# A state-space layer and a ternary feed-forward layer on eight cores: the state's mean, the weights' splits and the ternary weight passes put in another order

## The reference

```python
# first: a state-space layer with one averaged state kernel per state
xn = layernorm(layernorm(x)) * ln_g + ln_b        # the inner layer normalizes once more
x_proj, z = split(xn @ W_in.T + b_in);  z = silu(z)
B_proj = x_proj @ W_B.T * dt.mean()               # 16 states
A_mean = exp(t * log_A).mean(over channels)       # for every distance t
x_mean = causal_conv(B_proj, A_mean)              # over the whole sequence
y = (x_mean @ W_C.T + D_skip * x_proj) * z
y = y @ W_out.T + b_out + residual
# second: a feed-forward layer, 1024 -> 4096 -> 1024
h = silu(conv3(act_quant(x) @ weight_quant(w1).T))
h = act_quant(h) @ weight_quant(w2).T
```

## Time and profile before

| | |
|---|---|
| timed runs, slowest core | 1612.19 us median of 3 (1611.64 to 1612.52) |
| profiled execution | 1623.43 us, span of its slowest core (core 3) 1621.9 us |
| spans of the eight cores | 1594.0 to 1621.9 us |
| mean granted TensorE clock | 0.900 to 0.909 of full speed |
| TensorE matmuls busy | 1281.8 us (79%) |
| VectorE, ScalarE busy | 893.1 us (55%), 830.9 us (51%) |
| DMA | 206.30 MB, mean 127 GB/s |

### The profile page before, as it was taken

One profiled execution on the slowest core, in us unless ns is written; L12 is line 12 of the kernel. 1 busy time (PEld: TensorE's weight loads), 2 busy tenths in 40 slices (PEclk: granted clock), 3 DMA queues, 4 the chain that ended last, 5 costly groups with the idle time before them and its releaser, 6 DMA issues.

```text
span 1621.9 us, 23432 instructions; the slowest of 8 cores (1594.0 to 1621.9 us)
## 1 busy us (share of the span) xinstructions
PE 1281.8 (79%) x8148; PEld 790.3 (49%) x8148; DVE 893.1 (55%) x1461; ACT 830.9 (51%) x1118; POOL 83.4 (5%) x149
## 2 busy tenths in 40 slices
PE   2785799898983998887898745654698899889887
PEld 1262344565443755554566313443464566466433
DVE  1177412522036354545443424898898899789842
ACT  1334454678962234333334433886766667577531
POOL 0100000000000111111010000000000000000000
PEclk9768889898996999999999967997899999999999
DMA  9745668686245344654666582542001201010011
GB/s 272 203 146 130 192 187 255 191 271 186 96 136 153 118 143 140 177 148 148 143 167 131 162 226 98 169 156 91 1 1 53 79 1 50 30 53 27 26 66 65
DMA packets 86984, 206.30 MB, mean 127 GB/s; under 512 B 8495, under 2 KB 50783, under 8 KB 82692
## 3 DMA queue, kind: packets, MB, share of 16 engines
q1 hardware_dynamic: 62948, 99.41, 22.4%
q0 software_dynamic: 23920, 105.39, 20.6%
HBM read 170.99 MB, written 33.79 MB: 126 GB/s over the span
## 4 chain that ended last, share of the span: by engine, by line
PE 42%; DVE 16%; DMA 14%; ACT 11%; issue 11%; SPq 4%; POOL 1%; DVEq 0%; ACTq 0%; POOLq 0%
PE psum L893 10%; PE psum L857 10%; PE psum L734 7%; PE psum L694 6%; DMA b_wcb<-w_t 3%; PE psum L647 3%; DMA f_xr<-x_rev_t 2%; DMA f_wr<-w_in_t 2%; DMA f_lab<-s_logat 2%; DMA b_gz<-s_sz 2%; DVE b_h L1347 2%; PE psum L766 2%; DVE b_ev L1299 1%; DMA s_xq<-b_xqs 1%; DVE f_xt L1215 1%
## 5 line engine op out<-in xcount | busy, mean ns | idle before, releaser
L857 PE MATMUL psum<-b_xq,b_w1q 128*128 128x257 f16 x2048 | 261.8, 283 | 88.0 <-DVE b_ev L1299 79.4
L857 PEld LDWEIGHTS psum<-b_xq,b_w1q 128*128 128x128 fp8e4 x2048 | 203.5, 101 | 151.9 <-issue 108.1
L893 PE MATMUL psum<-b_w2q,b_hq 128*128 128x512 fp8e4 x1024 | 244.7, 389 | 8.1 <-DVE b_x2t L1384 8.1
L893 PEld LDWEIGHTS psum<-b_w2q,b_hq 128*128 128x128 f16 x1024 | 102.7, 100 | 116.9 <-issue 20.0
L1612 ACT ACTIVATE b_hs<-b_hs,c_cw 128x512 f32<-128x512 f32 x128 | 92.0, 719 | 56.6 <-DVE b_hs L1307 56.5
L1304 DVE SCALAR_TENSOR_TENSOR b_hs<-b_ev,c_cw,b_hs 128x512 f32<-128x512 f32 x128 | 95.1, 743 | 20.1 <-ACT b_hs L1608 20.0
L1307 DVE SCALAR_TENSOR_TENSOR b_hs<-b_ev,c_cw,b_hs 128x512 f32<-128x512 f32 x128 | 96.1, 751 | 13.3
L734 PE MATMUL psum<-f_xh,b_wxh 128*128 128x256 bf16 (+1 forms) x512 | 72.3, 287 | 35.0 <-DVE b_y L1261 28.2
L1608 ACT ACTIVATE b_hs<-b_ev,c_cw 128x512 f32<-128x512 f32 x128 | 90.3, 707 | 13.0 <-DVE b_ev L1299 13.0
L1299 DVE TENSOR_TENSOR b_ev<-psum,b_rbc 128x514 f32<-128x514 f32 x128 | 87.4, 685 | 1.1 <-PE psum L857 1.1
L1261 DVE SCALAR_TENSOR_TENSOR b_y<-psum,c_dsb,b_gz 128x256 f32<-128x256 f32 (+1 forms) x64 | 30.8, 482 | 98.5 <-PE psum L734 40.3
(11 more groups left out here) (223 smaller groups left out, 1968.2 us busy)
## 6 DMA issues: line engine op xcount, KB each, us to landing
f_xr<-x_rev_t POOLq DMA_DIRECT2D x15, 2048.0 KB, 12.5
f_pk<-w_t POOLq DMA_DIRECT2D x16, 1024.0 KB, 8.3
b_wca<-w_t POOLq DMA_DIRECT2D x32, 512.0 KB, 4.3
b_wcb<-w_t POOLq DMA_DIRECT2D x32, 512.0 KB, 5.1
b_wck<-w_t POOLq DMA_DIRECT2D x16, 1024.0 KB, 5.1
f_xt<-xo_t SPq DMA_DIRECT2D x5, 1640.0 KB, 11.4
s_sz<-f_o SPq DMA_DIRECT2D x40, 205.0 KB, 5.8
f_wr<-w_in_t SPq DMA_DIRECT2D x16, 512.0 KB, 6.2
```

What stands on the lines that cost most here:

```text
L857: e.matmul(psum[:, o:o + 257], sb_w1q.ap()[:, k * DH + mh * 128:k * DH + mh * 128 + 128], x[:, c:c + 257], start=k == 0, stop=k == KD - 1) ...
L893: e.matmul(ps[4 + (t % 2) * 2 + half], sb_hq[i].ap()[:, kh * 128:kh * 128 + 128], sb_w2q.ap()[:, kh * D + half * 512:kh * D + half * 512 + ...
```

## The change

Four things, in the order of the diff's effect on the program.

- *The state's mean.* At item 36 VectorE copies it out of PSUM ahead of the splits 16 and 17, with four copies of all 128 partitions instead of sixteen of 17 rows. SP's stores are issued at item 36, not 37: four for the body and two for the edge columns instead of twelve in all. `v_xmstack` at item 38 now stands ahead of that item's splits. The W_C stack's loads move from item 29 to 17 (waiting for `XN_V`, with another place in memory), its operations from item 31 to 21, and the load of the output bias from item 36 to 32.
- *Weights to split.* Portions 8 to 23 are loaded by GpSimd and not by SP, into three buffers and not two, so load j waits for split j - 3. GpSimd's ternary chunks start after split 22.
- *Ternary weight in portions.* The four chunks of a tile are no longer in a row at its end: on VectorE the passes 0 to 3 stand after the first gate, after the first low half, after the third low half and after `v_quant`; on ScalarE after `a_ln1`, after the second high half, after `a_xq` and after `a_quant`. The same holds for the sum of |w2|.
- *w1's loads.* The eight loads of the ternary w1 are issued three in tile 14, three in 15 and two in 16, each time after that tile's `s_xqst`.

```diff
-AT_WCT = 29
+AT_WCT = 17
...
             if i == AT_WCT:
-                e.wait_ge(*G_V.end())
+                e.wait_ge(*XN_V.end())
...
-            if i == 30:
-                for j in (8, 9):
-                    s_wr(e, j)
-            if i in SPLIT_AT:
-                for j in SPLIT_AT[i]:
-                    if j + 2 < 24:
-                        s_wr(e, j + 2)
+            if i == AT_WSUM:
+                e.wait_ge(*G_V.end())
+                e.dma_start(out=sb_bo.ap(), in_=d_bout).then_inc(*BOLD.dma())
             if i == AT_TOEP:
-                e.wait_ge(*Q_T.end())
-                e.dma_start(out=sb_bo.ap(), in_=d_bout).then_inc(*BOLD.dma())
-            if i == AT_TOEP + 1:
                 e.wait_ge(*XM_V.end())
                 for g in range(4):
...
-                    src = bass.AP(x.tensor, x.offset, [[4 * NQ, 1], [NQ, 4], [1, 1]])
-                    e.dma_start(out=capd(s_xm, g * TLOC, [[1, 1], [4 * TLOC, 4], [1, 1]]), in_=src,
-                                allow_slow_non_contiguous=True).then_inc(*XMST.dma())
-                    src = bass.AP(x.tensor, x.offset + 16 * 4 * NQ + 1, [[4 * NQ, 1], [NQ, 4], [1, 1]])
-                    e.dma_start(out=capd(s_xm, g * TLOC + TOWN + 1, [[1, 1], [4 * TLOC, 4], [1, 1]]), in_=src,
+                x = sb_xmt.ap()
+                for o, col in ((0, 0), (16 * 4 * NQ + 1, TOWN + 1)):
+                    src = bass.AP(x.tensor, x.offset + o, [[32 * 4 * NQ, 4], [NQ, 4], [1, 1]])
+                    e.dma_start(out=capd(s_xm, col, [[TLOC, 4], [4 * TLOC, 4], [1, 1]]), in_=src,
                                 allow_slow_non_contiguous=True).then_inc(*XMST.dma())
...
             if t == 14:
                 e.wait_ge(*GT_T.at("item", NIT - 1))
                 for k in range(2):
                     e.wait_ge(*WQST[k].end())
-                for j in range(8):
-                    e.dma_start(out=caps(sb_w1q, j * 512, ...), in_=capd(s_wq, j * 512, ...))
...
+            if 14 <= t <= 16:
+                for j in range((t - 14) * 3, min((t - 13) * 3, 8)):
+                    e.dma_start(out=caps(sb_w1q, j * 512, ...), in_=capd(s_wq, j * 512, ...))
...
+            if i == AT_TOEP:
+                e.wait_ge(*XM_T.end())
+                for q in range(4):
+                    e.tensor_copy(sb_xmt.ap()[:, q * NQ:q * NQ + NQ], qbank(q * 4)[:, 0:NQ]).then_inc(*XM_V.up())
+            if i == AT_TOEP + 2:
+                v_xmstack(e)
             if i in SPLIT_AT:
...
+            v_wtern(e, t, 0)
             if t:
                 v_ln1(e, t - 1)
             if items:
                 v_gate(e, items[1])
                 v_gatelo(e, items[0])
+            v_wtern(e, t, 1)
...
+    def v_wtern(e, t, j):
+        c = 4 * t + j
+        if c < NCC:
+            e.wait_ge(*WCKLD[c % 2].at("cast", c))
+            e.tensor_scalar(wcc_of(c), wcc_of(c), wscale(1), MAGIC, op0=ALU.mult, op1=ALU.add).then_inc(*QW_V.up("tern", c))
...
+    def a_wpass(e, t, j):
+        c = 4 * t + j
+        if c < NCC:
+            e.wait_ge(*QW_V.at("tern", c))
+            if c > 1:
+                e.wait_ge(*WQST[c % 2].at(c - 2))
+            e.activation(sb_wq8.ap()[:, (c % 2) * 1024:(c % 2) * 1024 + 1024], wcc_of(c), AF.Sign,
+                         bias=sb_cst.ap()[:, 0:1], saturate=False).then_inc(*QW_A.up("tern", c))
+        elif c < 2 * NCC:
+            c -= NCC
+            e.wait_ge(*WCKLD[c % 2].at("sum", c))
+            a_wabs(e, 2, c, wcc_of(c), 56 + c)
...
+        for j in range(8, 24):                      # GpSimd
+            if j < 10:
+                e.wait_ge(*WS_V.at(7))
+            elif j == 10:
+                e.wait_ge(*CO_V.end())
+            else:
+                e.wait_ge(*WS_V.at(j - 3))
+            e.dma_start(out=wr_of(j), in_=d_wout[:, (j - 8) * D:(j - 7) * D] if j < 16 else d_win[j - 16]
+                        ).then_inc(*WR2LD[wr_slot(j)].dma(j))
         for k in range(3):
             e.wait_ge(*XZ[k].end())
         e.wait_ge(*ST_V.at("xm"))
+        e.wait_ge(*WS_V.at(22))
```

More of the change, by code:

```diff
@@ L224, in write_program @@
     sb_xm32 = nc.alloc_sbuf_tensor_at("f_xm32", [80, TLOC], F32, offset=zone4)
-    sb_wc32 = nc.alloc_sbuf_tensor_at("f_wc32", [80, D], F32, offset=nc.lookup_mloc(sb_cf).addr)
-    sb_bo = nc.alloc_sbuf_tensor_at("f_bo", [33, D], F32, offset=nc.lookup_mloc(sb_q2).addr)
+    sb_wc32 = nc.alloc_sbuf_tensor_at("f_wc32", [80, D], F32, offset=nc.lookup_mloc(sb_q2).addr)
+    sb_bo = nc.alloc_sbuf_tensor_at("f_bo", [33, D], F32, offset=nc.lookup_mloc(sb_cf).addr)
+    sb_wr2 = nc.alloc_sbuf_tensor_at("f_wr2", [128, D], F32, offset=nc.lookup_mloc(sb_raw).addr)
     place[0] = base
@@ L349, in write_program @@
     WRLD, WS_V, WS_A = [sig("wraw_loaded0"), sig("wraw_loaded1")], sig("wsplit_vector"), sig("wsplit_scalar")
+    WR2LD = [sig(f"wraw2_loaded{k}") for k in range(3)]
     WM_V = sig("wscaled_vector")
@@ L530, in sync @@
                 s_xqst(e, (t - 3) // 2)
+            if 14 <= t <= 16:
+                for j in range((t - 14) * 3, min((t - 13) * 3, 8)):
+                    e.dma_start(out=caps(sb_w1q, j * 512, [[KD * DH, 128], [DH, KD], [1, 512]]),
+                                in_=capd(s_wq, j * 512, [[NCK * 2048, 128], [DH, KD], [1, 512]])).then_inc(*W1LD[j].dma())
         e.wait_ge(*XQST.end())
@@ L558, in s_xt, with wr_slot, wr_of, wr_loaded @@
                     in_=capd(d_xt, n * TC, [[KD * TLOC, 128], [TLOC, KD], [1, TC]])).then_inc(*XTLD[n % 2].dma(n))
+    def wr_slot(j):
+        return j % 2 if j < 8 else (j - 8) % 3
+    def wr_of(j):
+        return sb_wr2.ap() if wr_slot(j) == 2 else sb_wr.ap()[:, wr_slot(j) * D:wr_slot(j) * D + D]
+    def wr_loaded(j):
+        return (WRLD if j < 8 else WR2LD)[wr_slot(j)].at(j)
     def s_wr(e, j):
@@ L562, in s_wr @@
             e.wait_ge(*WS_V.at(j - 2))
-        src = d_win[8 + j] if j < 8 else d_wout[:, (j - 8) * D:(j - 7) * D] if j < 16 else d_win[j - 16]
-        e.dma_start(out=sb_wr.ap()[:, (j % 2) * D:(j % 2) * D + D], in_=src).then_inc(*WRLD[j % 2].dma(j))
+        e.dma_start(out=wr_of(j), in_=d_win[8 + j]).then_inc(*WRLD[j % 2].dma(j))
     def s_gz(e, q):
@@ L976, in vector @@
                 e.tensor_copy(sb_amt.ap(), ps[5][0:16, 0:128]).then_inc(*AM_V.up())
-            if i == AT_WCT + 2:
+            if i == AT_WCT + 4:
                 v_wcstack(e)
@@ L987, in vector @@
                     v_wlo(e, j)
[L988 to L995, removed]
         v_bout(e)
@@ L1011, in vector @@
                 v_gatelo(e, items[0])
+            v_wtern(e, t, 1)
+            if items:
                 v_gate(e, items[2])
@@ L1018, in vector @@
                 v_gatelo(e, items[2])
+            v_wtern(e, t, 2)
+            if items:
                 v_gatelo(e, items[3])
@@ L1021, in vector @@
                 v_quant(e, t - 1)
[L1022 to L1026, removed]
+            v_wtern(e, t, 3)
         v_wsum(e, 2)
@@ L1101, in v_wmul @@
     def v_wmul(e, j):
[L1103 to L1107, removed]
+        e.wait_ge(*wr_loaded(j))
+        w = wr_of(j).rearrange("p (k m) -> p k m", k=KD)
+        e.tensor_tensor(w, w, caps(sb_dbc, (j - 16) * 128, [[D, 128], [0, KD], [1, 128]]), op=ALU.mult
+                        ).then_inc(*WM_V.up(j))
     def v_wsum(e, wi):
@@ L1192, in v_wlo @@
     def v_wlo(e, j):
-        r = (j % 2) * D
         e.wait_ge(*WS_A.at(j))
-        e.tensor_tensor(split_of(j, 1), sb_wr.ap()[:, r:r + D], split_of(j, 0), op=ALU.subtract).then_inc(*WS_V.up(j))
+        e.tensor_tensor(split_of(j, 1), wr_of(j), split_of(j, 0), op=ALU.subtract).then_inc(*WS_V.up(j))
     def split_of(j, part):
@@ L1456, in scalar @@
                 a_ln1(e, t - 1)
-            for q in items[1:3]:
+            a_wpass(e, t, 0)
+            for q in items[1:2]:
+                a_gatehi(e, q)
+            a_wpass(e, t, 1)
+            for q in items[2:3]:
                 a_gatehi(e, q)
@@ L1464, in scalar @@
                 a_xq(e, t - 3)
+            a_wpass(e, t, 2)
             if t:
                 a_quant(e, t - 1)
[L1468 to L1478, removed]
+            a_wpass(e, t, 3)
         a_xq(e, 14)
@@ L1540, in a_whi @@
     def a_whi(e, j):
-        r = (j % 2) * D
-        e.wait_ge(*WRLD[j % 2].at(j))
+        e.wait_ge(*wr_loaded(j))
         if 2 < j < 8:
@@ L1549, in a_whi @@
             e.wait_ge(*WM_V.at(j))
-        e.activation(split_of(j, 0), sb_wr.ap()[:, r:r + D], AF.Copy).then_inc(*WS_A.up(j))
+        e.activation(split_of(j, 0), wr_of(j), AF.Copy).then_inc(*WS_A.up(j))
     def a_ab(e, n):
```

2 lines of the change are left out of this document (removed).

## The result

The changed kernel takes 1593.1 us (median) where the kernel before, run beside it, takes 1612.4: a ratio of 0.9873, 95% interval 0.9851 to 0.9895. That is about 20 us, and I had forecast 63; 1593 lies above my range of 1524 to 1577.

What follows compares the result with a forecast made beforehand. No engine was busy all the time; the chain of work changed engine through front, tile loop and tail. Gains 11.8 + 22.5 + 0 + 28.9 = 63.2; 1623.4 - 63.2 = 1560.2, less 11.2: 1549 us, 8-in-10 range 1524 to 1577.

Steps and rivals of the forecast that it cites:

- From the sum to the last gate, over SP's store and the load of z, 6.4.: Tile loop: from the sum with x to the tile's last gate takes 6.4 us, making 15.1 since gate 0.
- my own relay: Tile loop: chain from gate 0 through sum, last gate, activations and next chunk, 24.7 us, the length of a tile.
- the relay eats the tiles' gain: Rival, tile loop: z lands later beside chunks, each of 13 tiles 2 us longer, total 1575; chance 0.14.
- the 22.5: Tile loop: gain from ternary weight in portions, counted as 10.2 us in tiles 1 to 4 and 12.8 in 4 to 8.
- Tiles from 8 on, 0: Tile loop from tile 8: spread Abs passes cost by standing ahead what they cost by waiting; 0, bounds -8 and +10.
- The tail, 28.9: Last three tile steps: spreading w1's loads shortens 72.4 us to 43.5, gaining 28.9, bounds 18 and 32.4.
- one late pair of chunks: Tail: 3.5 us added to three steps of 40, as w1 loads share the DMA engines with chunks.
- a step without waits: Tail: 5.8 us to the sum with x plus 7.6 to the next step, 13.4; three steps are 40.
- The front, 11.8: Before the first gate: earlier mean and GpSimd weight loads bring that gate to 511, gaining 11.8 us, bounds 9 and 13.5.
- the mean's early copies: Front: four copies ahead of the splits get the mean out of PSUM at 476.8, 13.5 us earlier.
- Weights from GpSimd: Front: 512 KB loads land in 4.3 us from GpSimd, 4.8 from SP; late descriptors would cost 4.9 in all.
- The W_C stack at 0: Front: moving its loads and operations earlier costs 0, covered by VectorE's 4.96 us wait; without cover up to 6 lost.

Runs made afterwards that it cites:

- z ahead: Changed kernel, but SyncE issues the z of a tile's fourth item with the other three, before waiting for the sum with x: ratio 0.9543 to the kernel before.
- chunks held behind z: Changed kernel, but in tiles 1 to 6 GpSimd holds a tile's third and fourth chunks until its fourth gate is done: 1598.0 us in one execution.
- one edit: Kernel before the change, with SyncE issuing the fourth item's z together with the other three: ratio 0.9773, 37 us.
- no chunk beside w1: Changed kernel with z ahead, plus five Abs passes a tile in tiles 8 to 13 and two in 14, so steps 15 and 16 load no chunk: ratio 0.9458.
- two slots: Changed kernel with two slots instead of three for the weights that GpSimd fetches: 1607.9 us in one execution; copy of am to first gate 133.3 us.
- mean late: Changed kernel with the mean's copies and stack behind their items' splits again: 1618.9 us in one execution; copy of am to first gate 122.8 us.
- w1 late: Changed kernel with z ahead, one w1 piece in each of steps 14 to 16, the other five after the last full activations store: ratio 0.9536.

## Why the prediction was wrong, step by step

- **"From the sum to the last gate, over SP's store and the load of z, 6.4."** This is the step that failed. It measured 10.5, 10.0, 10.3, 10.2, 10.5, 10.8 and 9.8 in the first seven tiles (median of eight cores). I took the 6.4 from a tile in which no chunk was under way at that time; in my own relay the passes 0 and 1 release two chunks just ahead of it. I had this as a rival ("the relay eats the tiles' gain", 1575, chance 0.14), at 2 us a tile. It is 3.4 to 4.4 over my 6.4 in each of the first seven tiles, with the slow clock behind the stall on top, and 6.6 of the 22.5 are left. The runs with z ahead and with the chunks held behind z show it. (The two parts of the 22.5, 10.2 and 12.8, add up to 23.0; that slip decides nothing.)
- That last gate's wait in the earlier trace rows is put down to TensorE. I never asked how early z could be issued; the answer would have shown that z paces the kernel before as well (37 us by one edit).
- **Tiles from 8 on, 0.** Measured -3.5, within my bounds of -8 and +10.
- **The tail, 28.9.** Measured 17.3, under my bound of 18, and for another reason. I gave it to w1's loads, which alone give 2.3. The portions that I had left out of the tail give 9.5 alone. Of the missing 12, 4 are my base: I took the 72.4 of core 3, where the median core's three steps took 68.4. The rest is the term of 3.5 for "one late pair of chunks", which measured 51.2 - 40 = 11: w1's pieces and the chunks delay each other in two steps. My sum of a step without waits was right: with no chunk beside w1 three steps take 41.2, against my 40.
- **The front, 11.8.** Measured 10.3, right in size. But the reason I gave for half the way, the mean's early copies, carries nothing (the mean's way from its last copy to its stack took 16.0 us on the median core, 21.0 before, where I had 12.4); the end is set by the last loads, as the same paragraph had it, and these by the third slot.
- **Weights from GpSimd.** The loads of W_out and of the x half of W_in land in 5.4 and 6.0 us (median, core 3) from GpSimd, not in the 4.3 that I took; from SyncE in 4.8, and in 6.2 for both halves of W_in. With two slots the stretch is 133.3 on GpSimd and 133.1 before, so a cost of the move isn't seen; but those two kernels also differ in the mean's place, and the move was not undone alone. The rule of the Trainium skill (SBUF — State Buffer, "SBUF: two separate sides") that I weighed as speaking against the move shows nowhere in these numbers; they don't refute it either.
- **The first unit, not in my sum.** It loses 2.8 us. An earlier stack lets TensorE run ahead, stand 8.66 us and come back near the lower clock; with the mean late 2.2 of them come back.
- The W_C stack at 0: right as far as the rows go. The copy of am comes at 387.6 for 386.4, and between 383.4 and 389.8 in the other kernels, with the stack's move or without it.
- Open: the first feed-forward layer takes 520.4 to 522.3 us in ten of the eleven kernels with the changed front (the eleventh is the one with w1 late, 531.2), and 517.5 and 518.0 in the two without. Undoing w1's spread, the portions, the early mean or the third slot, each alone, doesn't bring it back; GpSimd as the queue and the places of the W_C and bias loads were not undone.

## What to carry to other kernels

When work is moved into a gap, list the transfers that it releases, and what else is issued within some 5 us of them: here two released chunks made the one load that everybody waited for some 3 us later, in each of the six tiles where the run without them can be compared. Before tuning around a load that ends a wait, ask from when on it could be issued; one line that moved it in its queue was worth 37 us alone and made the rest of the change worth four times as much in the loop. And undo each part by itself: the mean's early copies gave nothing, and the portions gave most of their gain in the tail, where I had counted none.

## What the runs showed of the hardware

An idle stretch of TensorE can cost more than its length: after 8.66 us and 6.01 us of waiting the next item ran at a granted clock of 0.52 and 0.57 and took some 2 us longer; after 1.52 us it ran at the full clock. Work that reaches an engine earlier can therefore make a stretch longer: 42.7 us from first gate to first sum with the mean early, 40.5 with it late. A load can land later beside others: a z load was there 8.4 us after its issue beside two 512 KB loads from GpSimd, and 5.8 with these held back. And a 512 KB load can hold up the queue that issues it: of w1's pieces three took 6.94 us to issue and the next three 14.22, in the run with z ahead (core 3).
